# A two-layer MLP in two passes, its first layer as seven block products in place of eight

## What is computed

```python
xn = _layernorm(x, g2, be2)
xm = xn * (1.0 + sc_m[:, None, :]) + sh_m[:, None, :]
h = jax.nn.gelu(xm @ W1 + b1, approximate=False)
x = x + gt_m[:, None, :] * (h @ W2 + b2)
```

## Time and profile before

| | us |
|---|---|
| median of 3 runs | 2166.5 (2166.19 to 2167.25) |
| span of the profiled execution | 2163.8 |
| TensorE, VectorE, ScalarE, GpSimd busy | 2126.4, 1290.6, 930.1, 958.5 |
| projection stage on TensorE | 1364.8 to 1459.3 |
| MLP on TensorE, starts | 1459.3 to 2159.5 |

### The profile page before, as it was taken

One profiled execution on the slowest core, in us unless ns is written; L12 is line 12 of the kernel. 1 busy time (PEld: TensorE's weight loads), 2 busy tenths in 40 slices (PEclk: granted clock), 3 DMA queues, 4 the chain that ended last, 5 costly groups with the idle time before them and its releaser, 6 DMA issues.

```text
span 2163.8 us, 30729 instructions
## 1 busy us (share of the span) xinstructions
PE 2126.4 (98%) x11326; PEld 1428.5 (66%) x11326; DVE 1290.6 (60%) x2872; ACT 930.1 (43%) x1780; POOL 958.5 (44%) x383
## 2 busy tenths in 40 slices
PE   8999999999999999999999999999999999999999
PEld 7888885444544445454544544778888888888887
DVE  5878877777777777777777756784312312122122
ACT  2111115566566666666666566435322222222221
POOL 2001007989799797988979784770000000000000
PEclk9999999999999999999999999999999999999999
DMA  7448347234361523625244324694201011011010
GB/s 287 180 156 265 134 168 186 49 89 107 70 143 47 122 55 76 142 65 132 51 95 94 70 70 135 202 326 156 97 1 59 15 44 59 1 59 59 1 39 20
DMA packets 129310, 223.29 MB, mean 103 GB/s; under 512 B 8574, under 2 KB 26054, under 8 KB 128968
## 3 DMA queue, kind: packets, MB, share of 16 engines
q1 hardware_dynamic: 108568, 180.43, 30.6%
q10 hardware_dynamic: 20592, 40.90, 5.0%
HBM read 146.31 MB, written 74.98 MB: 102 GB/s over the span
## 4 chain that ended last, share of the span: by engine, by line
PE 78%; POOL 11%; DVE 5%; issue 3%; DMA 2%; ACT 1%; SPq 0%; POOLq 0%; DVEq 0%; ACTq 0%; PEldq 0%
PE m_hid L1973 16%; PE p_acc L1987 16%; PE acc L861 12%; POOL psum_k L1208 10%; PE st L1453 9%; PE mx L1433 9%; PE o_ps L1470 9%; PE r_ps L1477 2%; DVE part L1313 2%; PE r_ps L1491 1%; PE p_acc L1952 1%; PE misc L815 1%; PE acc L839 1%; PE tp L825 1%; ACT prob L1252 1%
## 5 line engine op out<-in xcount | busy, mean ns | idle before, releaser
L1252 ACT ACTIVATE prob<-st 128x512 f32<-128x512 f32 (+3 forms) x1280 | 609.1, 540 | 374.3 <-PE st L1453 353.5
L1208 POOL TENSOR_TENSOR psum_k<-psum_k,prob 128x2048 f32<-128x2048 f32 (+1 forms) x150 | 663.9, 4426 | 20.7 <-ACT prob L1252 5.8
L1313 DVE TENSOR_REDUCE part<-mx 128x1 f32<-128x512 f32 x707 | 457.9, 685 | 75.0 <-PE mx L1433 70.6
L1453 PE MATMUL st<-q_st,k_st 98*128 98x512 f32 (+3 forms) x1280 | 491.0, 395 | 4.0 <-PE r_ps L1477 1.4
L1433 PE MATMUL mx<-k_st,qx_st 96*128 96x512 f32 (+3 forms) x1196 | 442.8, 395 | 10.3 <-DVE part L1313 2.8
L1453 PEld LDWEIGHTS st<-q_st,k_st 98*128 98x128 f32 x1280 | 241.3, 189 | 267.2 <-ACT prob L1252 152.3
L1874 DVE TENSOR_TENSOR m_g_lo<-m_g,m_g_hi 128x512 fp32r<-128x512 f32 x128 | 88.6, 692 | 479.7 <-ACT m_g_hi L1791 479.5
L1433 PEld LDWEIGHTS mx<-k_st,qx_st 96*128 96x128 f32 x1196 | 223.5, 189 | 129.9 <-DVE part L1313 60.4
L1470 PE MATMUL o_ps<-prob,v_sb 128*32 128x512 f32 (+3 forms) x2560 | 297.4, 539 | 3.7 <-POOL prob L1191 3.7
L1309 DVE CUSTOM_DVE_ANT_0 unused<-mx,mask_row 128x512 bf16<-128x512 f32 (+2 forms) x489 | 228.9, 486 | 119.0 <-PE mx L1433 109.0
L1784 ACT ACTIVATE m_g<-m_hid,vcol 128x512 f32<-128x512 f32 x128 | 88.3, 690 | 471.5 <-PE m_hid L1973 471.4
(11 more groups left out here) (186 smaller groups left out, 2529.2 us busy)
## 6 DMA issues: line engine op xcount, KB each, us to landing
k_st<-qk_scratch SPq DMA_DIRECT2D x96, 256.0 KB, 8.0
qx_st<-qk_scratch SPq DMA_DIRECT2D x96, 256.0 KB, 5.0
q_st<-qk_scratch SPq DMA_DIRECT2D x96, 256.0 KB
qk_scratch<-st_hi ACTq DMA_DIRECT2D x16, 1024.0 KB, 4.2
qk_scratch<-st_lo ACTq DMA_DIRECT2D x16, 1024.0 KB, 6.9
xs<-in_x_dram SPq DMA_DIRECT2D x8, 1024.0 KB, 8.9
v_sb<-v_scratch SPq DMA_DIRECT2D x8, 1024.0 KB, 15.6
o_scratch<-o_sb SPq DMA_DIRECT2D x32, 256.0 KB, 2.3
```

Of the source, the lines that this page charges most:

```text
L1208: nc.gpsimd.tensor_tensor(dst, src, prob[:, s % BUF, :, m:], ALU.add).then_inc(pool_added, 1)
L1252: nc.scalar.activation(prob[:, s % BUF, h, m:], st[n % RING][:, m:], ACT.Exp, scale=SCALE).then_inc(exp_done, 1)
L1313: nc.vector.tensor_reduce(most, bank[:, 0:w], AX.X, ALU.max).then_inc(mx_free, 1)
L1453: nc.tensor.matmul(st[n % RING][:, m:], k_st[u][0:MROWS, h, kt * P:(kt + 1) * P], q_st[0:MROWS, pos % 2, h, m:], start=True, stop=True).th ...
```

## The change

The MLP runs in two passes. The first makes all gelu tiles and stores them to a DRAM scratch `g`; the second loads them in order through a ring of eight tiles (`GB`), splits them again, and multiplies by the second weights.

In the first pass a pair of hidden tiles (rows) by a pair of chunks (columns), with the width 512 as two halves of 256, is a 2 by 2 by 2 block product. It is made by seven products of blocks in place of eight (`PRODUCTS`), each 2 times 3 matmuls. There are 32 such cycles, q = 0 to 31: eight weight sets (pairs of tiles) times four pairs of chunks. Four weight sets stand in SBUF at a time. The activation set, here *version*, changes every fourth cycle; version v has seven blocks (four raw, of which three are used as they are, and four sums). The weight sets 4 to 7 replace 0 to 3 from q = 16 on.

What each engine does anew: GpSimd makes the weights' block sums (`weight_sums`, 256 wide) and the activations' (`token_sums`, 1024 wide) for version 1 on; VectorE makes those of version 0 in the projection stage (`first_sums`). ScalarE takes the high parts (`x_high`, `weight_high`), copies products 1 and 7 out of PSUM (`copy`) and takes the gelu in place. VectorE takes the low parts (`x_low`, `weight_low`) and makes all sums of products: `u2`, `u4`, tiles 11, 12 and 21 from PSUM, `u3` and tile 22 in SBUF. The products take turns in six PSUM banks. A product waits until the one six before it has been drained, in the first cycle of a version for its low part, and in the first use of a weight set for that set's. SP reloads raw activations from `xm2` (2 MB, `load_raw`) once the last version is split, and each weight set in four loads of 128 KB.

```diff
+        self.g = dram("g_scratch", (HID, TOK))
...
@@ -1557,6 +1558,62 @@
         return Stage(sync, gpsimd, scalar, vector, tensor)
+PRODUCTS = (1, 6, 7, 5, 2, 3, 4)
+X_AT = {k: i for i, k in enumerate(PRODUCTS)}
...
+    def version(self, q):
+        return q // HALF
+    def weights(self, q):
+        return q // (HALF * SUPER) * HALF + q % HALF
+    def first_use(self, q):
...
+        WEIGHTS_AT = {1: 2, 2: 3, 14: 4, 16: 5, 17: 6, 18: 7}
...
+            def load_weights(w):
+                if w >= HALF:
+                    sp.wait_ge(product_done, R.done(4, HALF * SUPER - 2 * HALF + w))
+                else:
+                    sp.wait_ge(acc_ready, TT * (3, 6, 7, 7)[w])
+                if w >= 2:
+                    sp.wait_ge(w_summed, 4 * (w - 1))
+                if w:
+                    sp.wait_ge(w_loaded, 64 * w)
+                lo = w_raw[w % HALF]
+                for dst, row, half in ((block(lo, W_AT[1]), 0, 0), (block(lo, W_AT[2]), 0, 1), (a21[w % 2][:, :, :], 1, 0),
+                                       (block(lo, W_AT[4]), 1, 1)):
+                    at = (2 * w + row) * P
+                    sp.dma_start(dst, w1[half * 2 * P:(half + 1) * 2 * P, at:at + P].rearrange("(t p) n -> p t n", p=P)).then_inc(w_loaded, 16)
+            def load_raw(v):
+                first = 2 * (v % SUPER)
+                if v == 1:
+                    sp.wait_ge(acc_ready, TT * 5)
+                else:
+                    sp.wait_ge(x_split, len(PRODUCTS) * v)
...
+                for dst, half, n in zip(raw_x(v), (0, 1, 0, 1), (first, first, first + 1, first + 1)):
+                    sp.dma_start(dst, K.xm2[half * 2 * P:(half + 1) * 2 * P, cols(n)].rearrange("(t p) n -> p t n", p=P)).then_inc(raw_loaded, 16)
...
+            def store_g(it, q):
...
+                sp.wait_ge(activated, R.activated[it, q])
+                tile, n = 2 * R.weights(q) + row - 1, 2 * (R.version(q) % SUPER) + col - 1
...
+            for q in range(NQ + 1):
...
+                        load_g(i)
+                store_g((1, 1), q)
+                store_g((2, 2), q)
...
+                    load_w2(0)
+                if q % HALF == 0 and 2 <= q // HALF + 1 < NV:
+                    load_raw(q // HALF + 1)
+                if 0 <= q - (HALF * SUPER - HALF + 1) < HALF:
+                    load_weights(q - (HALF * SUPER - HALF + 1) + HALF)
+                if q == 19:
+                    sp.wait_ge(w_summed, 4 * PAIRS)
+                    sp.wait_ge(x_split, len(PRODUCTS))
+                    sp.wait_ge(w2_loaded, 16)
+                    load_w2(1)
...
+            def weight_sums(w):
...
+                s1, s2, s3, s4 = (block(lo, W_AT[k]) for k in (5, 6, 7, 3))
+                pool.wait_ge(w_loaded, 64 * (w + 1))
+                nc.gpsimd.tensor_tensor(s1, a21_, a22, ALU.add).then_inc(w_summed, 1)
+                nc.gpsimd.tensor_tensor(s3, a11, a21_, ALU.subtract).then_inc(w_summed, 1)
+                pool.wait_ge(w_summed, 4 * w + 1)
+                nc.gpsimd.tensor_tensor(s2, s1, a11, ALU.subtract).then_inc(w_summed, 1)
+                pool.wait_ge(w_summed, 4 * w + 3)
+                nc.gpsimd.tensor_tensor(s4, a12, s2, ALU.subtract).then_inc(w_summed, 1)
...
+            def token_sums(v, part):
...
+                        pool.wait_ge(y_stored[u], 16 * (NCH // 2 - 1))
+                elif part == 0:
+                    pool.wait_ge(x_split, len(PRODUCTS) * v)
+                for dst, a, b, after in x_sums(v)[2 * part:2 * part + 2]:
+                    if after:
+                        pool.wait_ge(t_summed, after)
+                    nc.gpsimd.tensor_tensor(dst, a, b, ALU.subtract).then_inc(t_summed, 1)
...
+            for q in range(NQ):
...
+                    token_sums(*SUMS[q])
+                if q < 2:
+                    weight_sums(q + 2)
+                if 13 <= q < 13 + HALF:
+                    weight_sums(q - 13 + HALF)
...
+            def x_high(v, k):
...
+                    act.wait_ge(product_done, R.done(k, HALF * v - 1))
+                if k in T_ORDER:
+                    act.wait_ge(t_summed, 4 * v + T_ORDER[k])
...
+                nc.scalar.activation(x_hi[:, X_AT[k], :, :], x_of(v, k), ACT.Copy).then_inc(x_hi_ready, 1)
...
+            def weight_high(w):
+                act.wait_ge(w_summed, 4 * (w + 1))
+                for part in (slice(0, 4), slice(4, 7)):
+                    nc.scalar.activation(w_hi[w % HALF][:, part, :, :], w_raw[w % HALF][:, part, :, :], ACT.Copy).then_inc(w_hi_ready, 1)
...
+            def copy(k, q, it):
+                act.wait_ge(product_done, R.done(k, q))
...
+                nc.scalar.activation(hid[it][q % 2][:, :], banks[R.bank(k, q)][:, :], ACT.Copy).then_inc(copied, 1)
...
+            def cycle(q):
+                gelu((2, 1), q - 1)
+                next_high(q - 1, 4)
+                copy(1, q, (1, 1))
...
+                if q < 2:
+                    modulate(NCH - 2 + q, 2)
+                    modulate(NCH - 2 + q, 3)
...
+                    w2_high(0, q - 20)
+                if 29 <= q < 32:
+                    for j in range(KT):
+                        w2_high(q - 28, j)
+                gelu((1, 1), q)
+                next_high(q, 2)
...
@@ -1802,35 +2126,22 @@
                 for t in range(KT):
...
+            def first_sums():
+                dve.wait_ge(y_ready, KT * 2 + 2)
+                for dst, a, b, after in x_sums(0):
+                    if after:
+                        dve.wait_ge(t_summed, after)
+                    nc.vector.tensor_tensor(dst, a, b, ALU.subtract).then_inc(t_summed, 1)
...
+            def x_low(v, k):
...
+                dve.wait_ge(x_hi_ready, len(PRODUCTS) * v + X_AT[k] + 1)
+                nc.vector.tensor_tensor(x_lo[:, X_AT[k], :, :], x_of(v, k), raw(x_hi[:, X_AT[k], :, :]), ALU.subtract).then_inc(x_split, 1)
...
+            def weight_low(w):
+                for n, part in enumerate((slice(0, 4), slice(4, 7))):
+                    dve.wait_ge(w_hi_ready, 2 * w + n + 1)
+                    nc.vector.tensor_tensor(w_lo[w % HALF][:, part, :, :], w_raw[w % HALF][:, part, :, :],
+                                            raw(w_hi[w % HALF][:, part, :, :]), ALU.subtract).then_inc(w_split, 1)
...
+            def add(k, q, dst, src):
+                dve.wait_ge(product_done, R.done(k, q))
+                nc.vector.tensor_tensor(dst[q % 2], banks[R.bank(k, q)][:, :], src[q % 2], ALU.add).then_inc(summed, 1)
...
+            def sum_u3(q):
...
+                nc.vector.tensor_tensor(hid[2, 1][q % 2][:, :], u2[q % 2], hid[2, 2][q % 2][:, :], ALU.add).then_inc(blended, 1)
...
+            def cycle(q):
+                sum_21(q - 1)
+                next_low(q - 1, 3)
+                next_low(q - 1, 4)
+                sum_u2(q)
+                next_low(q, 1)
+                next_low(q, 6)
+                sum_u4(q)
+                sum_u3(q)
+                if q == 0:
...
+                next_low(q, 7)
+                if q in WEIGHTS_AT:
+                    weight_low(WEIGHTS_AT[q])
...
+                    for j in range(KT):
+                        w2_low(q - 28, j)
+                sum_22(q)
+                sum_11(q)
+                next_low(q, 5)
...
-            for s in range(TT):
-                add_bias(0, s)
-            finish(0)
-            for n in range(1, NCH):
...
+            weight_low(1)
+            for q in range(NQ):
+                cycle(q)
+            g_low(0)
+            g_low(1)
+            sum_21(NQ - 1)
+            for i in range(2, HT * NCH):
...
+            def product(k, q):
...
+                elif before:
+                    p, r = before
+                    if p in (1, 7):
+                        pe.wait_ge(copied, R.copied(p, r))
+                    else:
+                        pe.wait_ge(summed, R.summed[{6: "u2", 5: "u4", 2: (1, 1), 3: (1, 2), 4: (2, 1)}[p], r])
+                if k == PRODUCTS[0] and R.first_use(q):
+                    pe.wait_ge(w_split, 2 * (R.weights(q) + 1))
+                if q % HALF == 0:
+                    pe.wait_ge(x_split, len(PRODUCTS) * R.version(q) + X_AT[k] + 1)
+                w, bank = R.weights(q) % HALF, banks[R.bank(k, q)]
+                for t in range(2):
+                    for e, (a, c) in enumerate(terms(w_hi[w][:, W_AT[k], t, :], w_lo[w][:, W_AT[k], t, :],
+                                                     x_hi[:, X_AT[k], t, :], x_lo[:, X_AT[k], t, :])):
+                        ins = nc.tensor.matmul(bank[:, :], a, c, start=(t == 0 and e == 0), stop=(t == 1 and e == 2))
+                ins.then_inc(product_done, 1)
...
+            for q in range(NQ):
+                for k in PRODUCTS:
+                    product(k, q)
+                    if q < 2 and k in (1, 7):
+                        for t in range(2):
+                            turn(NCH - 2 + q, 2 * (1, 7).index(k) + t)
+            for j in range(HT):
+                multiply(0, j)
```

643 lines of the change are left out of this document (413 added, 230 removed).

## The result

| | before | after |
|---|---|---|
| median, us | 2166.35 (4 runs beside it) | 2186.51 (2183.88 to 2187.82, 4 runs) |
| span of the profiled execution | 2163.8 | 2185.5 |
| last matmul starts | 2159.49 | 2181.20 |

The ratio is 1.0091, 95% interval 1.0076 to 1.0105: slower, by 20 us, where 13 us faster was forecast. It lies outside the range of 2137 to 2168.

What follows compares the result with a forecast made beforehand. TensorE, busy 98% of the span and never idle in the MLP, was taken as the bound. 43.5 us saved less 30.3 of costs gave 13.2 gained: span 2150.6, median 2153.3 us, range 2137 to 2168.

Steps and rivals of the forecast that it cites:

- The gain: First MLP layer: 1344 matmuls in place of 1536, 192 x 0.2266 = 43.5 us less; the second layer keeps 1536.
- Changes of the activation set: Every fourth MLP cycle VectorE's and ScalarE's queues get long: 2.5 us for five plain changes (0 to 8).
- All are in time, the last by 0.7 us: Change of activation set: VectorE's seven low parts end before TensorE asks for them, by a followed queue.
- rival B: VectorE and GpSimd block each other at every change; slower, about 2181 to 2191, or still about 2170; chance 0.12.
- DMA is nearly idle: Argument against late raw activations, and so against rival B: DMA moves only 44 GB/s in the MLP.
- Weight sets 4, 5, 7: First pass: sets ready late; waits of 4.2 us (set 4), 2.1 (set 5) and 2.5 (set 7).
- Start of the MLP: First product waits for weight set 0, split behind the last chunk's residual and statistics: 6.5 us (6 to 7.5).
- Cycles 0 and 1: In cycle 1 the last chunk's transposes wait for ScalarE's eviction behind cycle 0's gelus: 2.3 us (0 to 3).
- Between the passes: Pass two's first gelu tile is copied and split after two gelus of cycle 31: 2.5 us (2 to 3.5).
- Projection stage: Chunk 2's sums and chunk 3's lows delay VectorE's residuals; the two delays overlap: 5.5 us (1.5 to 11).
- The clock: One stretch of matmuls at 1.2 GHz behind a long stall, at MLP start or projection stage: 2.2 us (0 to 4.4).
- the prediction's own signs of being wrong: First product's wait below 5 us, stalls in every change, or 0.43 us starts behind more than one stall.

Runs made afterwards that it cites:

- e2: Kernel after, with 24 extra matmuls of 512 columns in TensorE's wait before the first product: 2182.77 us.
- e8: Kernel after, with 14 extra matmuls of 512 columns in TensorE's wait between the passes: 2183.85 us.
- e7: Kernel after, with the 28 token sums of activation sets 1 to 7 on VectorE, not GpSimd; loads as late as before: 2163.97 us.
- e4: Kernel after, with set 0's block sums and lows spread over later chunks and weight set 0's low ahead of the last residual: 2175.75 us.
- e3: Kernel after, with raw activations and weight sets 4 to 7 loaded ahead of their cycle's stores, not behind: 2170.07 us.
- e1: Kernel after, without GpSimd's token sums for versions 1 to 7; raw blocks stand in, so the result is not the reference's: 2161.22 us.
- e9: e6 with weight set 0 split before four last lows, last statistics behind them, and first two gelu tiles copied and split earlier in cycle 31: 2143.88 us.
- e11: e10 with the square root of the last chunk's variances moved behind ScalarE's evictions of cycle 0: 2142.90 us.
- e6: e5 with the 28 token sums of activation sets 1 to 7 on VectorE, not GpSimd: 2146.25 us.
- e5: Kernel after with the edits of e3 and e4, plus earlier token sums of set 1 and earlier stores of y: 2159.42 us.
- e10: e9 with weight set 5 split in cycle 15, not 16, and set 4's second pair of token sums in cycle 14: 2143.40 us.

## Why the prediction was wrong, point by point

- **The gain** was right: 1344 and 1536 matmuls, 43.5 us.
- **Changes of the activation set**: the step that failed by the largest factor. "All are in time, the last by 0.7 us" used the durations of VectorE's instructions alone; the row with the other end, 2.31 us at 1416.02, was seen and priced at 2.5 us for five changes. Measured 12.3. In cycle 8, where only 2.3 us of VectorE's queue were lost to GpSimd, the hand count nearly held (0.4 us). The rival B had the cause and the sign, with too small a chance, 0.12. That its 2170 to 2191 holds the result is in part luck: it charged 5 to 7 us at each of six changes and placed the collisions in the lows. The five plain changes cost 0.4 to 3.8 each, a low was stretched only at the first, and most of the rest came from the weight sets. "DMA is nearly idle" was read from the kernel before. What made the raw activations late was the queue: they were issued behind gelu stores that wait for ScalarE (and landed 9.8 us after their issue at 1617.63, where 7 had been taken), and set 1's sums waited for the last chunk's store.
- **Weight sets 4, 5, 7**: 8.8 forecast, 26.3 measured, half of the whole miss. The order of events was as told; the sizes were not, and for the same reason: splits and sums taken at their durations alone. The copy of set 4 held ScalarE for 8.19 us (until 1636.02), `w_lo` took 5.29 us for set 4, 3.13 for set 5 and 6.39 for set 7 in place of some 2.1, and each of the three was followed by a spell of half clock.
- **Start of the MLP**: 6.5 against 6.2, right. Where the chain was plain and GpSimd quiet, the count by hand held.
- **Cycles 0 and 1**: 2.3 against 2.1 is luck. The 2.3 were a wait of the last chunk's transposes in cycle 1; measured, cycle 1 loses 0.3. The rest is half clock behind the wait at the start: 1.9 us, which e2 took out of cycle 0.
- **Between the passes**: 2.5 forecast, 6.8 measured: the wait itself is 3.8, and 2.7 of the rest is half clock (e8).
- **Projection stage**: "I take 5.5 us" of 1.5 to 11; measured 11.6. "A stage that is already 5.5 us late loses little by the second" failed: the second wait was 3.69 us and had a spell of its own, and the stretch of the small instructions of `newton_rstd` was not costed at all.
- **The clock**: "I take one such loss, 2.2 us (0 to 4.4)". There were seven, 12.8 us. The size of one was about right; the number of waits was not, and half-clock starts behind more than one stall were among the prediction's own signs of being wrong. Two waits had been foreseen as long, and five more turned out so. The rule of the Trainium skill ("TensorE: Matmul & The Clock Gate", Part 1) that the prediction cited, and by which both foreseen stalls would pay, agrees with the trace: e8 prices one such spell at 2.7 us.
- **The bounds**: all high ends came to 55.4 us of cost and the real one is 65.3. The ends were taken as independent, but one cause, GpSimd at work beside VectorE, sat in five terms, and the clock multiplied them.
- **The Trainium skill's rule** on the port that VectorE and GpSimd share ("SBUF — State Buffer", "Who interferes with whom") had been cited as a rival's ground; the runs agree with it throughout: two-input SBUF instructions stretched (3.29 for 1.22), those with a PSUM input not (0.68).

By the table, the 35 us between forecast and measured budget are 27.3 in the changes of activation and weight sets, 6.1 in the projection stage and 4.3 between the passes, less 0.5 at the start and in cycles 0 and 1 and less the 2.2 that the forecast had set apart for the clock. By the runs, 22.5 us are gone once the token sums leave GpSimd (e7), with the clock lost behind those waits, and 10.8 with the order of the stage and of the start (e4). These can't be added up to the 35: much of the first can also be had back by early loads (e3, 16.4 us), which move the collisions to other places. How set 5's loss divides into a full queue and collisions stays open; with the token sums left out or on VectorE (e1, e7) cycles 16 and 17 still lost 9.6 and 9.8 us, against 8.6 in the kernel after.

## What to carry to other kernels

Before counting on an idle engine, ask what it shares with the busy one: by their own durations GpSimd's sums were free, and they cost 22 us by holding VectorE up, and moving them onto the busier engine won them back. Charge each TensorE wait of several microseconds with the clock behind it, and look for such waits in every stage that the change makes tighter. Removing one wait tells little until the engine behind it has slack: e9 to e11 moved one wait three times, while e6, with early loads, a spread stage and no token sum beside VectorE, won 40 us over the kernel after and 19 over the kernel before.

## What the hardware showed that was not expected

- A VectorE instruction of four columns took 1.22 us beside GpSimd against 0.16 alone, also when its only SBUF tile input is one (`TENSOR_SCALAR`, 1413.22; and four of 128x512 took 6.37 us against 1.92 in e5). So not only instructions with two SBUF inputs collide. The Trainium skill ("SBUF — State Buffer", "Who interferes with whom") names `tensor_scalar` among those that can; the rows agree.
- GpSimd is stretched as well: 3.44 us for 2.40, and 256 columns 1.71 us for 0.73 (at 1651.77).
- Over all thirteen traces, from 1360 us on: of 56 TensorE waits between 0.8 and 1.7 us none is followed by a spell of half clock, of 19 between 1.7 and 3.1 us eleven are, of 48 above that 47. The same wait in nearly the same kernel does both: 1.7 to 1.8 us at the same point of the stage was followed by 7 slow matmuls in e11 and by none in e10, and a wait of 3.8 us in e11 by none at all. A spell was mostly 5 to 12 matmuls at 0.43 us, 1 to 2.7 us; twice, in e5 and e9, it was eight transposes and two or three matmuls.
